# A DiT block with a routed expert layer on one core: the start of the kernel rewritten as one list per engine

## The chip, the cores and the metric

The kernel runs on 1 core of one Trainium2 chip. The metric is the device time of one execution in microseconds (us). Three runs of the kernel before took 1523.42, 1529.38 and 1528.04 us, median 1528.04.

## The reference

Everything is float32. Four batches of 1024 tokens with 256 features pass through two layers; each batch has a condition row and 77 context rows.

```python
m = silu(cond) @ w_ada + b_ada                    # nine sections of 256: shift, scale, gate x 3
h = ln(x) * (1 + sc_msa) + sh_msa
x = x + self_attn(h) * g_msa                      # 16 heads, windows of 128 tokens, shifted by 64
h = ln(x) * (1 + sc_mca) + sh_mca
x = x + topk_cross_attn(h, context) * g_mca       # 16 heads, softmax over the 16 largest of 77 scores
h = ln(x) * (1 + sc_mlp) + sh_mlp
x = x + swiglu(h) * g_mlp                         # hidden size 1024
nx = layer_norm(x, gamma, beta)                   # second layer
evidence = softmax(nx @ Wq @ (ctx @ Wk).T / 16) @ (ctx @ Wv)
combined = concat(nx, evidence, anchor)           # anchor: the condition row, the same for all tokens
routed = sum_e softmax(combined @ router_W + b)[e] * (silu(combined @ e_w1[e] + e_b1) @ e_w2[e] + e_b2)
g = sigmoid(silu(combined @ gate_w1 + gate_b1) @ gate_w2 + gate_b2)
out = x + g * (routed @ out_w + out_b)
```

## The kernel before

**Units and stages.** A unit is 256 tokens (two tiles of 128 rows); there are 16 units, four per batch. Each passes through stage A (self-attention up to the query of the cross-attention), stage C (cross-attention with its top-k) and stage B (gated MLP and experts). The loop body `both(k, r, batch)` works on B of unit k-1, C of unit k and A of unit k+1 at once. Ahead of the loop, A of units 0 and 1 and C of unit 0 must be done; a tail follows it.

**Order.** Every engine has its own instruction list, written by hand; engines meet at semaphores, and an engine that waits holds up all that is behind it on its list. The eight PSUM banks are shared by named jobs: `BANK_JOBS` gives each bank its jobs in order, and `before(name, u)` (L88) turns a name and a unit into the number of jobs that the bank had before. For the start this number comes from `PRO_ORDER` (L68 to 77), built from `FIRST_JOBS`. In the names below, `s00` to `s13` are the score jobs of stage A by tile and slot (4 slots of 4 heads), `p..` their turned probabilities, `c..` and `y..` the same of the cross-attention, `r1`, `r2` turned inverse sums.

**The start.** `prep_weights()` runs first, then `first()`, then `second()`, on TensorE (L476, L893, L935), DVE (L1727, L2073, L2106), ACT (L1330, L1346) and POOL (L1603, L1608). It holds:

- *Modulations.* TensorE turns 78 rows of biases and conditions into columns (L481), multiplies silu(cond) for four batches (4 columns of weights) with w_ada in slices of 512 columns (L488), so that the result has 4 rows and 2304 columns. DVE adds b_ada, loaded four times over, into `scores_or_ada` (L1759). Twelve transposes bring six sections to columns (L501), which DVE reads as `mods` (L1766). Gate rows are spread over 128 partitions by a product with a one-hot (L505, L520, L527) into `Gall`; POOL multiplies w_so and w_co with them (L1582). DVE multiplies the bias rows with the gates (L1774), then copies this batch's columns: modS, modC, chooseA (L1847 to L1849).
- *Bias rows in three parts.* A bias enters a token-major product as one bfloat16 product with three 16-bit parts of the row; `three_parts` (L1715) makes them on DVE: so, co, mo for four batches early, the expert rows late in `second()` (L1721 to L1724).
- *Folds.* The weights of the second layer are combined once: wk, wq turned and multiplied (MT, L559, L568), e_w2 turned (t.., L587) and multiplied with out_w (p.., L597), expert biases (b01, b2, L549), router rows (r0, r1), gates (G1 to G3, M0, M1), and the anchor's part of the first expert layer (L577, 28 products with 4 columns). They use banks 5 to 7 in turn, and DVE reads all of them, scaling some on the way, in the order of `FOLD_JOBS` (L367). One semaphore, `fold_read`, counts the reads.
- *Loads.* SP issues all of them (L380 to L439): columns, w_ada whole, x of unit 0, rows, the five attention weights, context, x of unit 1, fold weights, then (after the modulations, since they lie in the same tiles) Wm1 and W1nx, and later e_w2's third part, w_m2 and the evidence weights. w_ada borrows the tiles of W1nx and Wm1.

Stage A on TensorE is `a_turn_input` (L653), `a_k`, `a_q` (L668), `a_v` (L704), `a_scores` (L722), `a_turn_probs` (L730), `a_values` (L742), `a_turn_inverses` (L759), `a_project` (L676, L683), `a_turn_query`, `a_query`. DVE takes row maxima (L1928), ACT the exponents (L1249) and copies the turned slots (L1256). In stage C, `a_cross_scores` (L785) is copied by ACT (L1264), DVE finds the 16 largest (`a_topk`, half a and b, L1966 to L1978), POOL subtracts the maximum (`a_shift`, L1555), ACT takes the exponent (L1271), DVE keeps the chosen (`a_pick`, L1985). Stage B begins with `b_hidden` (L811), which reads hB.

## Time and profile before

| what | us |
|---|---|
| median of three runs | 1528.04 |
| the profiled execution | 1530.62 |
| its span, first to last instruction | 1528.8 |
| TensorE busy | 1456.4 (95%) |
| DVE busy | 1025.6 (67%) |
| ACT busy | 836.5 (55%) |
| POOL busy | 240.1 (16%) |
| mean granted TensorE clock | 0.968 of 2.4 GHz |

The difference of 1.8 us between the profiled execution and its span is time outside the first and last instruction. Busy shares are averages over the whole span. In the forty equal slices of the page, TensorE shows 5 in the second slice and 8 in the next three, then 9 up to the end; the granted clock reads 8, 8, 6, 6 in the first four slices and then 8 and 9.

### The profile page before, as it was taken

How to read it: one execution, taken by the hardware profiler on the slowest of the kernel's cores; microseconds unless marked ns; L12 is line 12 of the kernel's file. 1: busy time of each engine (PE TensorE's matmuls, PEld its weight loads, DVE VectorE, ACT ScalarE, POOL GpSimd, SP SyncE). 2: the span in 40 equal slices, each digit the busy share in tenths (PEclk: the TensorE clock that was granted, in tenths of full speed). 3: DMA queues.
4: the chain of work that ended last, by engine and by line, in shares of the span. 5: the costliest groups of instructions: out<-in, count | busy, mean ns of one | idle time of the engine just before them, and what ended most of it. 6: DMA issues, size and time to landing. Idle time of an engine off the chain costs nothing.

```text
span 1528.8 us, 32900 instructions
## 1 busy us (share of the span) xinstructions
PE 1456.4 (95%) x9793; PEld 1215.0 (79%) x9793; DVE 1025.6 (67%) x4678; ACT 836.5 (55%) x2546; POOL 240.1 (16%) x413
## 2 busy tenths in 40 slices
PE   5888699999999999999999999999999999999987
PEld 2656578888888888888888788888888888887876
DVE  4446685868768585867768585867768585857532
ACT  1415337574756537574756637484756637574423
POOL 2001210112123110111123110111123110111100
PEclk8866899999999999999999999999999999999999
...
DMA packets 25140, 31.70 MB, mean 21 GB/s; under 512 B 3051, under 2 KB 21627, under 8 KB 24443
## 3 DMA queue, kind: packets, MB, share of 16 engines
...
q14 instruction: 96, 0.79, 0.2%
...
## 4 chain that ended last, share of the span: by engine, by line
PE 73%; DVE 19%; issue 5%; ACT 1%; DVEq 1%; DMA 0%; POOL 0%; SPq 0%; POOLq 0%; ACTq 0%
PE bank L882 11%; PE bank L811 10%; PE bank L857 9%; PE bank L683 6%; DVE knocked L1978 5%; PE bank L864 5%; PE bank L821 5%; PE bank L668 4%; PE bank L742 4%; PE bank L730 4%; DVE M L1971 2%; PE bank L722 2%; DVE M L1966 2%; PE bank L676 2%; PE bank L639 2%
## 5 line engine op out<-in xcount | busy, mean ns | idle before, releaser
L811 PE MATMUL bank<-hB,Wm 128*128 128x256 f32 x1024 | 244.2, 385 | 3.7 <-issue 2.5
L811 PEld LDWEIGHTS bank<-hB,Wm 128*128 128x128 f32 x1024 | 191.9, 191 | 35.8 <-issue 11.9
L857 PE MATMUL bank<-nxT,W1nx 128*128 128x256 f32 x896 | 213.2, 384 | 0.0
L1249 ACT ACTIVATE prob<-bank,rmax 128x128 f32<-128x128 f32 x512 | 180.0, 435 | 32.9 <-DVE rmax L1928 32.9
L1256 ACT ACTIVATE probT<-bank 128x512 f32<-128x512 f32 (+1 forms) x256 | 141.4, 610 | 97.3 <-PE bank L795 76.0
L857 PEld LDWEIGHTS bank<-nxT,W1nx 128*128 128x128 f32 x896 | 167.2, 192 | 23.1 <-issue 2.8
L882 PE MATMUL bank<-W2p,gT 128*128 128x256 f32 x768 | 182.8, 381 | 0.0
L882 PEld LDWEIGHTS bank<-W2p,gT 128*128 128x128 f32 x768 | 144.0, 192 | 20.6
L1555 POOL TENSOR_TENSOR scores_or_ada<-scores_or_ada,M 128x308 f32<-128x308 f32 x128 | 94.8, 741 | 401.4 <-DVE knocked L1978 401.4
L1285 ACT ACTIVATE tbs<-bank,b1half 128x256 f32<-128x256 f32 x128 | 60.6, 473 | 150.9 <-PE bank L811 115.5
L1297 ACT ACTIVATE tbs<-bank,betaH 128x256 f32<-128x256 f32 x224 | 94.9, 484 | 85.7 <-PE bank L864 85.4
L1249 ACT ACTIVATION_READ_ACCUMULATOR prob<-bank,rmax 128x1 f32 x512 | 140.6, 276 | 0.0
L821 PE MATMUL bank<-Wm_g,gT 128*128 128x256 f32 x512 | 122.7, 380 | 0.0
L864 PE MATMUL bank<-wT,Vp 77*128 77x256 f32 x448 | 114.0, 383 | 0.0
L821 PEld LDWEIGHTS bank<-Wm_g,gT 128*128 128x128 f32 x512 | 96.9, 190 | 18.1 <-issue 4.2
L1978 DVE MATCH_REPLACE8 knocked<-M,scores_or_ada 128x77 f32<-128x77 f32 x512 | 108.5, 223 | 1.2 <-issue 0.8
L1978 DVE MATCH_REPLACE8 knocked<-M,knocked 128x77 f32<-128x77 f32 x512 | 108.5, 223 | 0.1
L864 PEld LDWEIGHTS bank<-wT,Vp 77*128 77x128 f32 x448 | 81.4, 190 | 14.3 <-issue 4.8
L1993 DVE SCALAR_TENSOR_TENSOR gT<-tbs,gT 128x256 f32<-128x256 f32 x128 | 55.8, 436 | 51.5 <-ACT gT L1287 51.4
L1928 DVE TENSOR_REDUCE rmax<-bank 128x4 f32<-128x512 f32 x128 | 80.7, 684 | 10.5 <-PE bank L722 10.5
L1966 DVE MAX8 M<-scores_or_ada 128x8 f32<-128x77 f32 x512 | 83.5, 225 | 4.1 <-ACT scores_or_ada L1264 4.0
L1971 DVE MAX8 M<-knocked 128x8 f32<-128x77 f32 x512 | 83.4, 225 | 0.2
...
## 6 DMA issues: line engine op xcount, KB each, us to landing
...
```

The costliest lines, as they stand in the source:

```text
L811: m = pe.matmul(bank_of(name)[:, half * UT:(half + 1) * UT], Wm1[:, k, c:c + P], hB[:, k, :], start=(k == 0), stop=(k == CB - 1))
L821: m = pe.matmul(bank_of("mo")[:, t * C:(t + 1) * C], gT[:, j, t * P:(t + 1) * P], Wm2_g[:, j, :], start=False, stop=(j == HJ - 1), skip_gr ...
L857: pe.matmul(bank_of(name)[:, n * UT:(n + 1) * UT], W1nx[:, k, c0 + n * P:c0 + (n + 1) * P], nxT[:, k, :], start=(n == 0 and k == 0), stop= ...
L864: m = pe.matmul(bank_of(name)[:, n * UT:(n + 1) * UT], Vp[:, c0 + n * P:c0 + (n + 1) * P], wT[:, :], start=False, stop=True, skip_group_ch ...
L882: m = pe.matmul(bank_of(name)[:, t * C:(t + 1) * C], hE[:, e % 2, k, t * P:(t + 1) * P], W2p[:, e * RB + k, :], start=False, stop=(k == RB ...
L1249: m = act.activation(prob[:, s, i, :], psum[s][:, i * P:(i + 1) * P], ACT.Exp, bias=rmax[:, t, s * HPS + i:s * HPS + i + 1], accum_out=rsu ...
L1256: act.activation(probT[0:np_, s], psum[s][0:np_, :].rearrange("p (i q) -> p i q", i=HPS), ACT.Copy)\
L1297: act.activation(tb[tb_of(name)][:, n * UT:(n + 1) * UT], bank_of(name)[:, n * UT:(n + 1) * UT], ACT.Tanh, bias=betaH[:, n0 + n:n0 + n + 1 ...
L1555: pool.tensor_tensor(Dx[:, t, g, :], S[:, t, g, :], M12[:, t, g, 0:1].to_broadcast([P, HPS, LC]), ALU.subtract)\
L1966: dve.max(M12[:, t, h, 0:8], S[:, t, h, :]).then_inc(topk, 1)
L1971: dve.max(M12[:, t, h, 8:TOPK], K[:, h, :]).then_inc(topk, 1)
L1978: dve.match_replace(K[:, h, :], top, src, KNOCKED).then_inc(topk, 1)
```

## The change

The first two units and all weight folds become one list per engine, `prologue()`, with an order of single slots instead of groups; `PRO_JOBS` gives the banks' order to match. The modulations are made by feature: w_ada is the stationary side, siluT (4 columns) the moving one, so they come out as columns; only the three gate sections are still made as rows. w_ada is loaded in two pieces, sections 0 and 1 first. The loads follow first use. Folds rotate through the three banks in a new order and are read by DVE or ACT, each bank with a semaphore of its own; scale factors that the reads applied are now put on out_w and the gate row once. `three_parts` moves to POOL. The loop and the tail are as before.

The diff of the fold order and of the loads, with the semaphores that SP waits on:

```diff
-ada_loads = [(Wada[k], w_ada[k * P:(k + 1) * P, :]) for k in range(CB)]
+ada_loads = [(Wada[k][:, 0:2 * C], w_ada[k * P:(k + 1) * P, 0:2 * C]) for k in range(CB)]
+ada_rest_loads = [(Wada[k][:, 2 * C:9 * C], w_ada[k * P:(k + 1) * P, 2 * C:9 * C]) for k in range(CB)]
...
+FOLD_JOBS = [
+    "cols", "mS", "cT", "cK", "cV", "g25", "g8", "bv", "G0", "mR", "t01", "t00",
+    "wq", "M0", "p01", "anchor", "p00", "t11", "t10", "b01", "p10", "p11", "G1", "b2",
+    "t20", "t21", "p21", "p20", "G2", "wk", "MT", "G3", "r0", "M1", "r1",
+]
...
+    sp.dma_start(Wqkv[:, :, :], blocks(w_qkv)).then_inc(qkv_loaded, 16)
+    load_ctx(0)
+    sp.dma_start(Wkv[:, :, :], blocks(w_kv)).then_inc(kv_loaded, 16)
+    for loads, loaded in ((ada_rest_loads, ada_rest_loaded), (rows_loads, rows_loaded), (gated_loads, gated_loaded)):
         for dst, src in loads:
             sp.dma_start(dst, src).then_inc(loaded, 16)
-    load_ctx(0)
+    sp.dma_start(Wq2[:, :, :], blocks(w_q)).then_inc(q2_loaded, 16)
     load_x(1, 1)
     for dst, src in folded_loads:
         sp.dma_start(dst, src).then_inc(folded_loaded, 16)
     sp.dma_start(ew2[:, :, :], e2_rows[:, 0:2 * RB, :]).then_inc(ew2_loaded, 16)
     for dst, src in anchor_loads:
         sp.dma_start(dst, src).then_inc(anchor_loaded, 16)
-    sp.wait_ge(init_full, 6)
+    sp.wait_ge(fold_full, max(FOLD_FULL[n] for n in ("g8", "g25", "mR")))
     for dst, src in wb_loads:
         sp.dma_start(dst, src).then_inc(wb_loaded, 16)
-    sp.wait_ge(fold_read, FOLD_JOBS.index("t01") + 1)
+    wait_read(sp, "t00")
+    wait_read(sp, "t01")
     sp.dma_start(ew2[:, 0:RB, :], e2_rows[:, 2 * RB:3 * RB, :]).then_inc(ew2_loaded, 16)
     load_x(2, 2)
     load_x(3, 3)
-    sp.wait_ge(fold_read, FOLD_JOBS.index("b2") + 1)
+    wait_read(sp, "anchor")
+    for dst, src in evidence_loads:
+        sp.dma_start(dst, src).then_inc(evidence_loaded, 16)
+    for name in ("b01", "b2", "MT", "p20", "p21"):
+        wait_read(sp, name)
     load_wm2()
-    sp.wait_ge(fold_read, FOLD_JOBS.index("anchor") + 1)
-    for dst, src in evidence_loads:
-        sp.dma_start(dst, src).then_inc(wb_loaded, 16)
...
```

The modulations on TensorE, new:

```python
def modulations(name, sections):
    pe.wait_ge(silu_ready, 1)
    if name == "mS":
        pe.wait_ge(ada_loaded, 16 * CB)
    else:
        pe.wait_ge(ada_rest_loaded, 16 * CB)
    bk = fold_bank(name)
    for n, sec in enumerate(sections):
        for f in range(CB):
            c, o = sec * C + f * P, (n * CB + f) * NB
            for k in range(CB):
                m = pe.matmul(bk[:, o:o + NB], Wada[k][:, c:c + P], siluT[:, k, :], start=(k == 0), stop=(k == CB - 1))
    m.then_inc(fold_full, 1)
def gate_sections(name, gates):
    pe.wait_ge(ada_rest_loaded, 16 * CB)
    bk = fold_bank(name)
    for n, g in enumerate(gates):
        c = (3 * g + 2) * C
        for k in range(CB):
            m = pe.matmul(bk[0:NB, n * C:(n + 1) * C], siluT[:, k, :], Wada[k][:, c:c + C], start=(k == 0), stop=(k == CB - 1))
    m.then_inc(fold_full, 1)
```

TensorE's new list (in place of `prep_weights`, `first`, `second`), after which the loop begins:

```python
def prologue():
    columns_turned()
    modulations("mS", (1, 0))
    context_turned(0, fold_bank("cT"))
    a_turn_input(0)
    context_keys(0, fold_bank("cK"))
    pe.wait_ge(qkv_loaded, 16)
    a_v(0, 0)
    a_q(0)
    a_v(1, 0)
    a_k(0)
    context_values(0, fold_bank("cV"))
    gate_sections("g25", (0, 1))
    gate_sections("g8", (2,))
    a_scores(0, range(SLOTS), 0)
    value_biases()
    fold_gates(0)
    modulations("mR", (4, 3, 7, 6))
    a_turn_probs(0, 0, 0)
    a_turn_probs(0, 1, 0)
    a_turn_probs(0, 2, 0)
    fold_turn_second(0, 1)
    a_turn_probs(0, 3, 0)
    fold_turn_second(0, 0)
    fold_turn("wq", wq_sb)
    fold_mlp_gates(0)
    a_scores(1, range(SLOTS), 0)
    a_values(0, 0)
    fold_second(0, 1)
    a_turn_probs(1, 0, 0)
    fold_anchor()
    a_turn_probs(1, 1, 0)
    a_turn_probs(1, 2, 0)
    a_turn_probs(1, 3, 0)
    a_turn_inverses("r1", "pv", 0)
    fold_second(0, 0)
    a_values(1, 0)
    fold_turn_second(1, 1)
    fold_turn_second(1, 0)
    fold_expert_biases("b01", (0, 1))
    pe.wait_ge(prepared, 1)
    pe.wait_ge(doneA, 3)
    pe.wait_ge(gatedA, 2)
    a_project("pv", oT, "so", Wso_g, 0)
    fold_second(1, 0)
    fold_second(1, 1)
    fold_gates(1)
    a_turn_query(0)
    fold_expert_biases("b2", (2,))
    fold_turn_second(2, 0)
    fold_turn_second(2, 1)
    pe.wait_ge(q2_loaded, 16)
    a_query(0)
    fold_second(2, 1)
    a_turn_input(1)
    fold_second(2, 0)
    pe.wait_ge(readA, 2)
    a_cross_scores(0, range(SLOTS), 0)
    fold_gates(2)
    fold_turn("wk", wk_sb)
    a_v(0, 1)
    a_k(1)
    a_v(1, 1)
    fold_qk()
    fold_gates(3)
    a_cross_scores(1, range(SLOTS), 0)
    fold_router_anchor()
    a_q(1)
    a_scores(0, range(SLOTS), 1)
    a_turn_probs(0, 0, 1)
    a_turn_probs(0, 1, 1)
    fold_mlp_gates(1)
    a_turn_probs(0, 2, 1)
    a_turn_probs(0, 3, 1)
    a_scores(1, range(SLOTS), 1)
    a_values(0, 1)
    a_turn_probs(1, 0, 1)
    a_turn_probs(1, 1, 1)
    fold_router_rows()
    a_turn_probs(1, 2, 1)
    a_turn_probs(1, 3, 1)
    a_turn_inverses("r1", "pv", 1)
    a_values(1, 1)
    a_turn_picked(0, 0, 0)
    a_turn_picked(0, 1, 0)
    a_turn_picked(0, 2, 0)
    a_turn_picked(0, 3, 0)
    a_project("pv", oT, "so", Wso_g, 1)
    pe.wait_ge(values_read, 1)
    a_cross_values(0, 0)
    a_turn_picked(1, 0, 0)
    a_turn_picked(1, 1, 0)
    a_turn_picked(1, 2, 0)
    a_turn_picked(1, 3, 0)
    a_turn_inverses("r2", "xv", 0)
    a_cross_values(1, 0)
    pe.wait_ge(doneC, 1)
    pe.wait_ge(gatedC, 2)
    a_project("xv", oT2, "co", Wco_g, 0)
    a_turn_query(1)
    a_query(1)
    turn("ln3", xnB, 0, normed[2], TILES)
    wait_folds(pe)
    pe.wait_ge(wb_loaded, 16 * len(wb_loads))
    pe.wait_ge(evidence_loaded, 16 * len(evidence_loads))
    pe.wait_ge(prepared_b, 1)
    pe.wait_ge(prepared, 2)
```

POOL's, with `three_parts` as it now runs there (`chain` waits for the instruction it wraps):

```python
def three_parts(np_, r0, r1, nth):
    n = r1 - r0
    cur = rows[0:np_, r0:r1, :]
    part, rest = split_b[0:np_, 0:n, :], split[0:np_, 0:n, :]
    for p in range(3):
        chain(pool.tensor_copy(part, cur))
        last = pool.tensor_copy(bias3[32 * p:32 * p + np_, r0:r1, :], part)
        if p < 2:
            chain(last)
            chain(pool.tensor_tensor(rest, cur, part, ALU.subtract))
            cur = rest
    last.then_inc(prepared, 1)
    pool.wait_ge(prepared, nth)
def prologue():
    rstd_of(0, EPS0, 0)
    pool.wait_ge(rows_gated, 1)
    three_parts(NB, 0, 3, 1)
    wait_read(pool, "G0")
    wait_read(pool, "bv")
    gate_so(0)
    rstd_of(0, EPS0, 1)
    gate_co(0)
    a_spread("pv", 0)
    rstd_of(1, EPS0, 0)
    pool.wait_ge(expert_rows, 1)
    three_parts(1, BIAS.index("e0"), len(BIAS), 2)
    a_shift(0, 0, 0)
    a_shift(0, 1, 0)
    a_shift(0, 2, 0)
    a_shift(0, 3, 0)
    a_shift(1, 0, 0)
    a_shift_kept(0, 0)
    a_shift(1, 1, 0)
    a_shift(1, 2, 0)
    a_shift(1, 3, 0)
    a_spread("pv", 1)
    a_shift_kept(1, 0)
    rstd_of(1, EPS0, 1)
    a_spread("xv", 0)
    rstd_of(2, EPS0, 0)
```

DVE's, cut to what the prediction speaks of; the rest follows the same jobs:

```python
def prologue():
    dve.wait_ge(fold_full, FOLD_FULL["cols"])
    read_done("cols", dve.tensor_copy(cols[:, :], fold_psum("cols")[:, 0:NCOL]))
    a_load(0, 0)
    ln_stats(0, xs[0], 0)
    silu()
    helpers()
    ln_apply(0, xs[0], xnA, 0)
    dve.wait_ge(fold_full, FOLD_FULL["mS"])
    read_mods("mS", 0, (1, 0))
    context_turned(0, fold_psum("cT"))
    dve.tensor_copy(modS[:, :], mods[:, 0, 0:4]).then_inc(doneA, 1)
    context_keys(0, fold_psum("cK"))
    ...
    a_load(1, 0)
    ln_stats(0, xs[1], 1)
    a_max(0, (0,), 0)
    a_max(0, (1,), 0)
    a_max(0, (2,), 0)
    dve.wait_ge(rows_loaded, 16 * len(rows_loads))
    dve.wait_ge(fold_full, FOLD_FULL["bv"])
    so_co = rows[:, 0:2, :].rearrange("b n c -> b (n c)")
    read_done("bv", dve.tensor_tensor(so_co, fold_psum("bv")[0:NB, :], so_co, ALU.add))
    a_max(0, (3,), 0)
    gate_bias_rows()
    read_fold("G0", Gall[:, 0:2, :].rearrange("p g c -> p (g c)"), fold_psum("G0")[:, :])
    dve.wait_ge(fold_full, FOLD_FULL["mR"])
    read_mods("mR", 2, (4, 3, 7, 6))
    read_fold("t01", e2T[1], fold_psum("t01")[:, :])
    dve.tensor_copy(modC[:, :], mods[:, 0, 4:8]).then_inc(doneA, 1)
    read_fold("t00", e2T[0], fold_psum("t00")[:, :])
    dve.wait_ge(folded_loaded, 16 * len(folded_loads))
    dve.tensor_scalar(outw, outw, 0.25, None, ALU.mult).then_inc(out_scaled, 1)
    ...
    dve.tensor_copy(chooseA[:, :], choose[:, 0, :]).then_inc(doneA, 1)
    prep_c(0)
    a_invert_sums(0)
    ...
    prepared_for_b()
    dve.wait_ge(fold_full, FOLD_FULL["b01"])
    expert_bias("b01", (0, 1))
    a_residual(xs[0], xs[0], "so", 0)
    wait_drained(dve, "so", 0)
    ln_stats(1, xs[0], 0)
    ...
    halve_expert_biases()
    read_fold("p21", W2p[:, 2 * RB + 2:2 * RB + 4, :].rearrange("p k c -> p (k c)"), fold_psum("p21")[:, :])
    read_fold("p20", W2p[:, 2 * RB + 0:2 * RB + 2, :].rearrange("p k c -> p (k c)"), fold_psum("p20")[:, :])
    a_topk("a", 0, 0, 0)
    a_topk("a", 0, 1, 0)
    a_topk("b", 0, 0, 0)
    a_topk("a", 0, 2, 0)
    a_topk("a", 0, 3, 0)
    a_topk("b", 0, 1, 0)
    a_topk("b", 0, 2, 0)
    a_pick(0, 0, 0)
    a_bias_queries(1)
    a_topk("a", 1, 0, 0)
    a_topk("b", 0, 3, 0)
    a_max(0, (0,), 1)
    ...
```

ACT keeps its jobs in nearly the same order, with ten fold reads among them: wq after the first four turned slots; t11, p10 and p11 after r1; t21 ahead of the query bias; G2, wk, MT and G3 around the cross-attention scores; M1 after the first turned slots of unit 1. Its exponent of the first half of tile 0 (`a_cross_exp(0, 0, 0)`) stands after `a_keys(1)` and ahead of `a_copy_values(1)` and the read of MT.

## Rows read from the trace of the kernel before

**Rows 1.** Windows: from:to, us, busy per engine (instructions), clock, DMA share, GB/s.

```profile
0.00:13.10 13.10, 0.36 (x1) 0.20 (x2) 3.03 (x15) 1.49 (x2) 3.82 (x13) 1.00 0.55 206
13.10:42.30 29.20, 24.91 (x90) 13.04 (x90) 17.11 (x42) 3.54 (x7) 4.29 (x6) 0.82 1.07 351
42.30:104.50 62.20, 50.30 (x305) 37.67 (x305) 25.20 (x55) 19.39 (x81) 2.60 (x6) 0.79 0.13 40
104.50:177.20 72.70, 51.59 (x363) 41.29 (x363) 45.97 (x239) 31.66 (x106) 14.65 (x24) 0.71 0.07 26
177.20:1528.80 1351.60, 1329.21 (x9039) 1122.78 (x9039) 934.33 (x4328) 780.46 (x2351) 214.79 (x365) 0.99 0.04 11
```

**Rows 2.** Timeline (start us, us, what), TensorE: first matmul of the loop.

```profile
177.16 3.35 PE L811 MATMUL bank<-hB,Wm 128*128 128x256 f32 x7 [1.26 <-ACT hB L1210]
```

**Rows 3.** Chain that ended last, in order of time: start us, us, what.

```profile
5.41 7.57 DMA Wm<-in_L_xcond_w_ada_dram
13.11 10.04 PE bank L488 x20
...
118.10 10.39 PE bank L577 x56
```

**Rows 4.** DMA issues: KB each, us from issue to landing.

```profile
Wm<-in_L_xcond_w_ada_dram SPq DMA_DIRECT2D x1, 1152.0 KB, 7.6
```

**Rows 5.** Timeline of DVE and ACT: first statistics, first modulation.

```profile
15.06 0.75 DVE L1900 BATCH_NORM_STATS2 stat<-x 128x6 f32<-128x256 f32 x2 [6.21 <-DMA x<-in_x_dram]
...
30.94 1.02 ACT L1210 ACTIVATE hA<-bank,modS 128x256 f32<-128x256 f32 x2 [23.72 <-DVE chooseA L1849]
```

**Rows 6.** Timeline of TensorE: the first scores.

```profile
42.27 1.15 PE L722 MATMUL bank<-km,qT 32*128 32x256 f32 x16
```

**Rows 7.** Timeline of DVE: first top-k, expert rows split, last residual.

```profile
104.55 0.66 DVE L1966 MAX8 M<-scores_or_ada 128x8 f32<-128x77 f32 x4 [4.04 <-ACT scores_or_ada L1264]
...
159.53 0.62 DVE L1721 CAST split_b<-Vp 1x1024 bf16<-1x1024 f32 x1
...
165.17 0.42 DVE L1722 COPY bias<-split_b 1x1024 bf16<-1x1024 bf16 x1
...
170.49 0.69 DVE L1953 TENSOR_TENSOR x<-x,bank 128x512 f32<-128x512 f32 x1 [4.18 <-PE bank L683]
```

**Rows 8.** Windows inside the 56 records of L577, columns as in rows 1.

```profile
118.10:120.00 1.90, 1.90 (x18) 1.90 (x18) 1.90 (x4) 1.18 (x7) 0.00 (x0) 0.97 0.00 0
120.00:122.00 2.00, 2.00 (x11) 2.00 (x11) 2.00 (x14) 2.00 (x13) 0.00 (x0) 0.50 0.00 0
```

**Rows 9.** Timeline of SP's queue: the old load of all nine bias rows.

```profile
7.69 0.49 SPq L420 DMA_DIRECT2D scores_or_ada<-in_L_xcond_b_ada_dram  x1
```

**Rows 10.** Timeline of TensorE: jobs that price the list.

```profile
23.85 1.03 PE L495 MATMUL bank<-Wco_g,bv 128*4 128x256 f32 x4
...
65.80 1.04 PE L587 MATMUL bank<-ident,gT 128*128 128x128 f32 x8
66.67 1.91 PE L730 MATMUL bank<-ident,prob 128*128 128x128 f32 x16
...
72.40 1.08 PE L742 MATMUL bank<-probT,va 128*32 128x128 f32 x32
```

**Rows 11.** Window: the busiest part of the second stretch, columns as in rows 1.

```profile
60.50:81.90 21.40, 20.36 (x129) 15.90 (x130) 8.17 (x14) 5.39 (x21) 0.74 (x2) 0.92 0.17 51
```

**Rows 12.** Timeline of POOL: two products, two copies.

```profile
27.49 1.82 POOL L1582 TENSOR_TENSOR Wso_g<-Wso_g,Gall 128x256 f32<-128x256 f32 x2 [10.07 <-DVE Gall L1770]
...
67.12 0.74 POOL L1576 COPY xnA<-rinv 128x256 f32<-128x256 f32 x2 [36.27 <-DVE rinv L1933]
```

**Rows 13.** Timeline of DVE: the bias rows of four batches, split.

```profile
27.45 2.14 DVE L1774 TENSOR_TENSOR Vp<-Vp,scores_or_ada 4x256 f32<-4x256 f32 x3
...
30.82 0.54 DVE L1721 CAST split_b<-Vp 4x768 bf16<-4x768 f32 x1
...
35.29 0.35 DVE L1722 COPY bias<-split_b 4x768 bf16<-4x768 bf16 x1
```

632 lines of the change are left out of this document (316 added, 316 removed), and 9 rows, old and new, of the table PRO_JOBS.

## The prediction

> **What bounds the kernel now.** I read the windows first. They cut the span at four marks: 42.3 us (first scores), 104.5 us (first top-k), 177.2 us (first matmul of the part that the loop repeats) and the end [rows 1]. From 177.2 us on TensorE is busy 1329.2 of 1351.6 us at a granted clock of 0.99: no room there, and the change touches none of it. Ahead of that mark it is busy 127.2 of 177.2 us at 0.71 to 0.82. So the change is worth what it does to the moment at which line 811 first runs with hB, 177.16 us [rows 2], and everything behind moves with it.
>
> Then the chain of waits, for what holds each stretch [rows 3]. TensorE waits until 13.1 us for the second half of w_ada and then spends 10.0 us on the modulations of all nine sections. The DMA issues price that wait: 1152 KB, behind as much again, landed 7.6 us after issue [rows 4]. DVE meets x only at 15.06 us, as x queues behind them, and copies modS, modC and chooseA last; ACT starts to modulate when the third is done, at 30.94 us [rows 5]. The first scores start at 42.27 us [rows 6]. Top-k starts at 104.55 us; from 159.53 to 165.6 us DVE splits four expert bias rows, with the oT product behind it on the queue, and the residual of "co" at 170.49 us is late by as much [rows 7]. TensorE gives 10.4 us to the anchor fold ahead of the turned probabilities of unit 1 [rows 3]. Within that fold the clock falls from 0.97 to 0.50 while TensorE shows no gap [rows 8].
>
> **Part 1, up to the first scores.** Removed ahead of the first modulation: seven ninths of the w_ada bytes, the 36 KB load of b_ada for four batches [rows 9], ten products of 512 or 256 columns, twelve transposes, five reads, and the gate and row products that sit before modS. SP's queue gains four issues (w_ada and b_ada in pieces) at 0.4 to 0.5 us, but Wqkv and Wkv move ahead of them. New path: the first 512 KB of w_ada are issued where the 2304 KB were. The 2304 KB took 7.6 us [rows 4], so 512 KB and the 256 KB of x take a third of that plus the time to start, which I estimate as landing at 10 us. DVE now has the statistics of x ahead of silu: 10.0 + 1.1 (stats and aggregates, from 15.06 to 16.2) + 0.35 = 11.5 us. "mS" is 8 products, 16 records. No earlier row has such products except the anchor's: 18 records in 1.90 us at 0.97, so 0.106 each, 11 in 2.00 us at 0.50, so 0.182 or more each [rows 8]: 1.7 to 3.0 us. With 0.8 us for reading them and copying modS, ACT starts at 15 to 16.5 us; I take 15.7, 15.2 earlier than now.
>
> From there to the scores took 11.3 us [rows 5, 6]. The same work stays, less 0.9 us of context keys that now fit into the wait for ACT, plus 12 records for the gate sections. Four records of 256 columns take 1.03 us with the tail that the next one covers, 0.86 from start to start [rows 10]: 2.6 us. First scores at 15.7 + 13.0 = 28.7 us, 13.6 earlier. Bounds: 26.5 (every column at full clock) and 31.
>
> **Part 2, first scores to first top-k: 62.2 us now.** TensorE's list there in records: 96 of 256 columns (bv, G0, G1, M0, b01, b2, six expert folds, so, q2) at 0.215 = 20.6 us; 72 transposes (eight slots, wq, six turns of e_w2, r1, ln2, ln1) at 0.11 [rows 10] = 7.9; three score groups 3.2 and two value groups 2.1 [rows 6, 10]. That is 33.8 us at full clock. "mR" and the anchor are 88 four-column records: 9.3 us at 0.106, 16.4 at the 0.187 that the whole anchor fold averaged (10.46 us for 56). MT, wk, both router jobs, G2, G3 and M1 leave this stretch. Since the wide work fills the waits, I take the clock of its busiest part, 0.92 [rows 11]: 36.7 + 16.4, and 3 us of waits in place of 11.9 = 56. First top-k at 28.7 + 56 = 85 us. Ends: 43.1 (all at full clock, no wait) and 67 (the clock of now, 0.79, on the wide work, 42.8, with 16.4 and 8 of waits). ACT takes ten fold reads that were DVE's, at about 0.6 each, five here and five in part 3: it was busy 19.4 of 62.2 and 31.7 of 72.7 us [rows 1], so they cost nothing unless they stand in front of a copy that TensorE wants; then one costs 0.6.
>
> New heads of queues. DVE waits for Wm1, W1nx and the rest (4.5 MB) ahead of "b01"; SP issues them only after "mR", at about 38 us (28.7, then scores, bv, G0 and mR) instead of 25. At 351 GB/s [rows 1] they land at 51; DVE gets there at about 57. Cost nothing, up to 5 us if the list runs faster than I think. POOL now splits the bias rows, and gate_so, rstd of unit 1, gate_co and the spread of the inverse sums queue behind it. No row shows POOL on so few partitions. The nearest are a product of 128x256 in 0.91 us and a copy in 0.37 [rows 12], 3.6 and 1.45 ns per column: for 768 columns 2 x 2.7 + 6 x 1.1 = 12 us, against 4.8 on DVE, from 30.82 to 35.64 [rows 13]. It starts near 36 us (28.7, four maxima, bv and the row products: 7); with two gates, rstd and the spread (5.2 together) the last ends near 53. The inverses are wanted at 50 to 54, when the anchor lets the slots be turned. I take zero, with 6 as the other end.
>
> The Trainium skill (GPSIMD Engine Reference, section 4.1 Engine selection) speaks against this move: element work belongs on VectorE, two inputs being about twice as slow on GpSimd and one input about equal. The rows differ for two inputs: 3.6 ns per column on POOL [rows 12] against 2.8 on DVE with 4x256 [rows 13] or 1.35 with 128x512. By the page the first split would take some 7 us in place of my 12, and the sum stays.
>
> **Part 3, first top-k to the loop: 72.7 us now.** Two things leave the chain: the split (159.53 to 165.6, 6.1 us) and the anchor (10.4) [rows 3, 7]. That gives 56.2. DVE has 46.0 us of work there now [rows 1], 39.5 without the split and the anchor's read, so the floor is that plus the tail that nothing shortens, 6.7 us from the residual at 170.49 to 177.16, less the 3.5 of it that is DVE work counted already: 43. Added to TensorE in this stretch are MT, wk, router, G2, G3 and M1, some 5 us, in waits of 21 us. The other end is 66.6, where only the split is saved, because the scores of unit 1 wait for a query bias that DVE now does after the first pick. That pick waits for ACT's exponent, which waits for two shifts on POOL, which stand behind the second split: 1024 columns, 16 us by the same prices, begun near 76 us, 9 before the top-k. It ends near 92, shifts and exponent at 94; the pick is due seven top-k groups (9.8 us) after 85. So it just fits, and 6 us is the price if it doesn't. First loop matmul: 85 + 56 = 141 us, against 177.2: **36 us saved**.
>
> **The loop and its loads.** w_m2 is issued after MT is read, about 95 us; its gating wants it at about 138. Evidence weights go before it and are earlier than now. Nothing there changes the loop.
>
> **The sum.** The profiled execution took 1530.62 us (span 1528.8), 2.6 above the median of 1528.04. 1530.6 - 36.2 = 1494.4; against the median 1491.8. I say 1491.5.
>
> **Rivals.** (a) *The clock holds.* Part 2 is then 43.1 + 3, and part 3 is 52, since some 14 us of TensorE work on its chain ran at 0.71: first top-k at 75, loop at 127, 50 saved: 1478. For it: busier stretches now have more clock (0.92 against 0.79) [rows 1, 11]. Against it: the clock fell inside the anchor fold with TensorE never idle [rows 8]. The Trainium skill (TensorE: Matmul & The Clock Gate, What's actually happening) has the clock follow how busy TensorE was, which would give this case; the trace disagrees for four-column products, of which the new list has 104 in place of 56. (b) *The gain is half.* In-order queues collide: part 2 keeps 8 us of waits and takes 67, part 3 takes 62: loop at 158, 19 saved: 1509. Against it, 21 us of DVE idling and 12 of TensorE's have a visible cause that the order removes. (c) *POOL becomes the bound, slower than before.* Place: the second split, in front of the first shift. At 16 us it is covered; each microsecond above 17 delays everything in part 3. From 36 us above that, 53 in all or 3.3 times the rows' price (casts to bfloat16 appear in no row of POOL), the kernel is slower; at four times, the second split alone makes it 1539. (d) *The order does nothing*: loads alone bring the first scores forward and the waits move to the same weights later. Only 4.5 MB are issued later than now and they are covered, so this is unlikely: 1525.
>
> **Chances.** Forecast (28 to 44 saved) 0.58; (a) 0.16; (b) 0.18; (c) 0.03; (d) 0.05, half of it within 0.5%, which is 7.6 us and about what a measurement of this kernel can tell from no change. Faster by more 0.94, within 0.03, slower 0.03. The range reaches to both (a) and (b), leaving their far halves out: 1473 to 1510.
>
> **What would show it.** Right: ACT's first modulation at 15 to 17 us, first scores by 31, first top-k near 85, the loop at 135 to 147, and its length still 1351 us; no DVE casts of bias rows. Wrong: POOL's splits above 17 us each with the first shift behind them, a DVE wait on the loads of Wm1 ahead of "b01", a clock at 0.5 over long busy stretches, or a loop that is longer than 1352 us, which no step here allows.

## The result, and the profile after the change

Four runs of the changed kernel took 1487.58 to 1492.47 us, median 1489.76; the kernel before, its first three runs and one more, had a median of 1526.22. The ratio is 0.976, 95% interval 0.974 to 0.978. The change saves 36.5 us; 36.2 were forecast, and 1489.8 us stands against the 1491.5 on record. The profiled execution took 1487.95 us with a span of 1485.9.

That agreement to 0.3 us is luck. Between the two profiled executions the spans differ by 42.9 us, of which 38.9 lie ahead of the loop; the profile of before was 4.4 us above its median, the one of the changed kernel 1.8 below its own. The windows of the changed kernel, cut at its own marks (first scores, first top-k, first matmul of the loop), to be read against [rows 1]:

```profile
0.00:27.80 27.80, 16.77 (x71) 13.24 (x71) 8.41 (x33) 5.04 (x9) 4.76 (x15) 1.00 0.79 253
27.80:81.80 54.00, 54.00 (x374) 45.15 (x373) 25.02 (x61) 23.14 (x86) 19.53 (x23) 0.84 0.49 170
81.80:138.30 56.50, 42.72 (x341) 32.55 (x339) 39.64 (x228) 33.89 (x111) 18.03 (x27) 0.85 0.06 20
138.30:1485.90 1347.60, 1326.08 (x9039) 1118.70 (x9039) 933.10 (x4328) 781.57 (x2351) 215.53 (x366) 1.00 0.04 11
```

Part 1 went from 42.3 to 27.8 us, part 2 from 62.2 to 54.0, part 3 from 72.7 to 56.5. In part 2 TensorE is busy in every microsecond, where it idled 11.9; what limits it there is its own work and its clock. In part 3 it still idles 13.8 us. The loop is 38.9 us earlier than at [rows 2].

The loop itself reads 1347.6 us against 1351.6, with the same 9039 matmuls. Some 1.8 us of that lie at its entry: its first eight records took 3.78 us before and 1.99 here, the lower clock level against the upper. For the rest I have no cause in the change. In the experiments below, whose loop has the same instructions, this stretch took 1347.6 to 1353.9 us from profile to profile; I count the rest as spread, without two profiles of one kernel to show it. For the same reason the marks, not the medians, decide about differences of a few microseconds.

The timeline of the changed kernel (start us, us, what), TensorE and then DVE, ACT: first modulations, first scores, anchor fold, loop; first statistics; first modulation by ACT:

```profile
11.39 0.59 PE L542 MATMUL bank<-siluT,W1nx 128*128 128x4 f32 x2 [4.76 <-DVE siluT L1892]
11.85 0.57 PE L542 MATMUL bank<-siluT,Wm 128*128 128x4 f32 x2
...
27.82 1.15 PE L780 MATMUL bank<-km,qT 32*128 32x256 f32 x16
47.04 8.40 PE L633 MATMUL bank<-condT,W1ev 128*128 128x4 f32 x56
138.29 0.91 PE L869 MATMUL bank<-hB,Wm 128*128 128x256 f32 x3 [1.26 <-ACT hB L1298]
```
```profile
9.92 0.75 DVE L2009 BATCH_NORM_STATS2 stat<-x 128x6 f32<-128x256 f32 x2 [2.93 <-DMA x<-in_x_dram]
```
```profile
16.31 1.02 ACT L1298 ACTIVATE hA<-bank,modS 128x256 f32<-128x256 f32 x2 [9.08 <-PE bank L711]
```

The chain that ended last, its start (start us, us, what). The load of x and the modulations stand where the load of w_ada and ten microseconds of line 488 stood [rows 3]. POOL's second split is on it as a whole, all eight steps from 75.63 to 86.5 us, and behind it two shifts, the exponent and the copies that ACT has queued behind that:

```profile
6.98 2.80 DMA x<-in_x_dram
11.39 3.58 PE bank L542 x16
...
75.63 1.04 POOL split_b L1744
...
82.23 2.13 POOL tbs L1748
```

The timeline of POOL: the first step of each split, the last step of the second, and the first shifts behind it:

```profile
34.04 0.81 POOL L1744 CAST split_b<-Vp 4x768 bf16<-4x768 f32 x1 [21.75 <-DVE nxT L1921]
...
75.63 1.03 POOL L1744 CAST split_b<-Vp 1x1024 bf16<-1x1024 f32 x1 [4.75 <-DVE Vp L1937]
...
85.50 1.04 POOL L1745 COPY bias<-split_b 1x1024 bf16<-1x1024 bf16 x1
86.62 2.03 POOL L1682 TENSOR_TENSOR scores<-scores,M 128x308 f32<-128x308 f32 x3
```

Eight steps take 8.7 us for 768 columns and 10.9 for 1024. The three shifts in one record behind the second split are the sign of a queue that has built up: POOL is late for all three.

### The profile page after: what moved, and what is told of

Same layout as the page of the kernel before. It is cut to its first block, busy times and chain, and to the rows that moved or that the text cites. A ratio compares the mean times of both kernels' runs of the same rounds, so it can differ in the third digit from the quotient of the medians.

```text
span 1485.9 us, 32998 instructions
## 1 busy us (share of the span) xinstructions
PE 1439.6 (97%) x9821; PEld 1209.6 (81%) x9821; DVE 1006.2 (68%) x4648; ACT 843.7 (57%) x2556; POOL 257.8 (17%) x429
## 4 chain that ended last, share of the span: by engine, by line
PE 81%; DVE 12%; issue 4%; POOL 1%; ACT 1%; DVEq 0%; SPq 0%; DMA 0%; POOLq 0%; ACTq 0%
PE bank L915 12%; PE bank L940 11%; PE bank L869 10%; PE bank L922 6%; PE bank L741 6%; PE bank L879 5%; PE bank L800 4%; PE bank L788 4%; PE bank L726 4%; DVE knocked L2087 4%; PE bank L853 3%; PE bank L780 2%; PE bank L734 2%; DVE M L2075 2%; PE bank L697 2%
## 5 line engine op out<-in xcount | busy, mean ns | idle before, releaser
L1682 POOL TENSOR_TENSOR scores<-scores,M 128x308 f32<-128x308 f32 x128 | 94.5, 739 | 371.1 <-DVE knocked L2087 371.0
L2087 DVE MATCH_REPLACE8 knocked<-M,scores 128x77 f32<-128x77 f32 x512 | 108.4, 223 | 0.7 <-issue 0.7
L1674 POOL TENSOR_SCALAR vare<-mv 128x2 f32<-128x2 f32 x64 | 14.0, 220 | 406.5 <-DVE mv L2013 404.0
L2075 DVE MAX8 M<-scores 128x8 f32<-128x77 f32 x512 | 83.5, 224 | 1.5 <-issue 0.7
```

The lines of the kernel that those rows point to most:

```text
L1682: pool.tensor_tensor(Dx[:, t, g, :], S[:, t, g, :], M12[:, t, g, 0:1].to_broadcast([P, HPS, LC]), ALU.subtract)\
L2075: dve.max(M12[:, t, h, 0:8], S[:, t, h, :]).then_inc(topk, 1)
L2087: dve.match_replace(K[:, h, :], top, src, KNOCKED).then_inc(topk, 1)
```

## The experiments

All are read at four marks, taken from each kernel's own timelines in us:

```
                              ACT modulates  scores  top-k    loop   loop to end
before                            30.94       42.27  104.55  177.16    1351.6
after                             16.31       27.82   81.78  138.29    1347.6
splits on DVE again               16.44       27.39   81.32  145.35    1353.9
old order of the loads            25.23       35.79   89.74  146.33    1349.9
all folds read by DVE             16.17       27.25   82.01  140.67    1351.6
anchor fold twice                 16.10       27.92   93.01  149.62    1350.1
silu first                        15.07       27.10   81.07  137.62    1347.6
expert rows early                 15.95       27.38   79.68  134.85    1351.4
anchor in parts                   16.01       28.18   72.53  127.13    1350.3
folds behind the so product       16.36       27.88   87.72  142.94    1349.7
the three together                14.88       26.93   76.58  131.85    1350.9
the same, rstd first              14.81       26.88   72.81  129.80    1348.2
the same, context first           13.89       27.62   73.57  129.93    1350.6
before, second split on POOL      31.22       42.66  106.05  175.25    1349.5
```

### The splits on DVE again

```diff
 # DVE
     gate_bias_rows()
+    three_parts(NB, 0, 3)
...
+    dve.wait_ge(expert_rows, 1)
+    three_parts(1, BIAS.index("e0"), len(BIAS))
     a_normalise("xv", oT2, 0)
 # POOL: both calls removed
```

> Both splits of the bias rows back on DVE, the second just ahead of the oT product. My theory (the move to POOL took them off DVE's path): the first costs DVE 4.9 us ahead of the reads of G0, mR and the turned e_w2, of which 2 to 4 reach TensorE; the second costs 6.1 on DVE's chain, and gives back the 1 to 2 us that POOL's second split now holds up ACT at 75 to 89 us. First loop matmul 6 to 9 us later than 138.3. Rival (they would be covered anyway, since DVE has 4 to 6 us waits): 0 to 2 us later. Rival (POOL is now the bound): 1 to 2 us earlier.

1500.76 us, ratio 0.983 (0.980 to 0.985): 7.1 us later than the changed kernel at the loop, and not at the top-k (0.5 earlier). So the first split is free on either engine, where 2 to 4 us were expected of it. The second, on DVE, is in front of the oT product as before [rows 7] (timelines of DVE, then TensorE):

```profile
126.02 0.67 DVE L1917 CAST split_b<-Vp 1x1024 bf16<-1x1024 f32 x1
...
131.56 0.42 DVE L1918 COPY bias<-split_b 1x1024 bf16<-1x1024 bf16 x1
132.01 0.69 DVE L2059 TENSOR_TENSOR oT<-bank,oT 128x512 f32<-128x512 f32 x1
```
```profile
133.23 3.62 PE L741 MATMUL bank<-Wco_g,oT 128*128 128x256 f32 x8
...
139.49 3.75 PE L726 MATMUL bank<-hA,Wq 128*128 128x256 f32 x8 [0.75 <-ACT hA L1298]
```

Less than half of the 7.1 us is the split itself: the oT product starts at 132.01 us and not at 128.88, 3.1 later, since it would have waited for TensorE in part anyway. The rest is clock. Behind the pause of 5.2 us TensorE ran at a granted 0.50 from 132.8 us to the loop, at 1.00 in the changed kernel, and the two groups above took 3.62 and 3.75 us where they take 1.89 and 1.96 there.

### The old kernel with its second split on POOL

```diff
 # POOL, first()
     rstd_of(0, EPS0, 1)
+    pool.wait_ge(expert_rows, 1)
+    three_parts(1, BIAS.index("e0"), len(BIAS), 2)
 # DVE, second()
-    three_parts(1, BIAS.index("e0"), len(BIAS))
     a_normalise("xv", oT2, 0)
```

> The kernel before with one part of the change alone: the second split of bias rows on POOL, behind rstd of unit 1. Theory: DVE's 6.1 us ahead of the oT product go and POOL's 11 us fit between 90.6 and 106: loop 5 to 6 us before 177.2. Rival (the parts only pay together, another wait takes its place): under 2 us.

1528.22 us, ratio 1.000 (0.999 to 1.002), and the loop only 1.9 us earlier. Part 3 is 3.5 us shorter, but the top-k comes 1.5 us later. The oT product did not move (timelines of DVE and TensorE of this kernel):

```profile
100.73 1.45 DVE L1937 TENSOR_SCALAR xnA<-x,mv,rstd 128x256 f32<-128x256 f32 x2
...
165.50 0.69 DVE L1967 TENSOR_TENSOR oT<-bank,oT 128x512 f32<-128x512 f32 x1 [3.68 <-PE bank L743]
```
```profile
156.05 3.75 PE L669 MATMUL bank<-hA,Wq 128*128 128x256 f32 x8 [0.75 <-ACT hA L1212]
```

DVE is free but TensorE is not ready. In the kernel before, the product that oT reads had been there since 162.65 us (its timeline of TensorE):

```profile
161.57 1.08 PE L742 MATMUL bank<-probT,vc 77*32 77x128 f32 x32
```

So 3.0 of the split's 6.1 us could be won there at most. Here even these were lost: the query took 3.75 us where the kernel before took 1.97, at a granted clock of 0.56 to 0.59 from 154 to 162 us, and the same product ended at 165.44. What was won is 2 us in the co product behind, which no longer starts after a pause of 3.8 us. Whether the clock was lower by the edit or by chance, one profile does not say.

Of the 1.5 us at the top-k 0.4 are there already at the first scores. The rest has a cause that neither theory had. While POOL splits (90.9 to 102.0 us), two jobs of DVE take longer: the copy of chooseC 0.77 us and not 0.18, the normalisation at 100.73 1.45 us and not 0.73. The run with rstd first, below, shows the same. So the same move is worth 0 to 2 us in the old order and 7 in the new one.

### The old order of the loads

```diff
 # SP
+    (ada_rest_loads)
     load_x(0, 0)
-    Wqkv; load_ctx(0); Wkv; ada_rest_loads
     rows_loads; gated_loads
+    Wqkv; Wkv; Wq2; load_ctx(0)
-    Wq2
```

> Order of the loads as before (all of w_ada, then x, rows, so and co, then Wqkv, Wkv, Wq, context), with all else new. Theory: x lands at 14 to 15 us instead of 9.9 and silu stands behind it on DVE, and Wqkv lands near 19; mS starts at 16, first scores 4.5 to 6 us later, and the delay runs through to the loop undiminished: first loop matmul 4.5 to 6 later. Rival (slack behind the first scores swallows it, as folds fill the waits): first scores late by 5, loop late by less than 2.

1497.42 us, ratio 0.982 (0.979 to 0.984). ACT's first modulation comes 8.9 us later, and each later mark 8.0: nothing on the way takes the delay up, and it is larger than the 4.5 to 6 that I had expected. x reaches DVE at 16.84 us and not at 9.92, and silu stands behind its statistics, so TensorE's modulations wait for x; behind them TensorE waits another 1.85 us, for the context, which the old order loads last (timeline of TensorE):

```profile
18.32 0.59 PE L544 MATMUL bank<-siluT,W1nx 128*128 128x4 f32 x2 [11.78 <-DVE siluT L1894]
...
23.73 0.52 PE L663 MATMUL bank<-ident,ctx_sb 77*128 77x77 f32 x2 [1.85 <-DMA ctx_sb<-in_ctx_dram]
```

The context, needed ahead of the turn of xnA, is what sets ACT's start here. So of the 14.5 us that part 1 gained, some 8 would be lost again with the old loads under the new lists. How the gain splits between loads and modulations under the old lists, this run does not show.

### All folds read by DVE

```diff
 # ten read_fold calls go from ACT's list to DVE's, each near its old place
-    act: read_fold("wq", ...), "t11", "p10", "p11", "t21", "G2", "wk", "MT", "G3", "M1"
+    dve: the same
```

> All ten fold reads of ACT put back on DVE, at the places where their jobs fall. Theory: DVE is the denser engine from 81.8 us on; five reads of 0.6 there cost 2.5 to 3.5 us at the loop, the five before cost 0 to 1. Rival (ACT's queue was the one that held things, as the chain of waits runs through its reads of MT and G3 at 89 to 90 us): loop within 1 us of 138.3 or earlier.

1494.26 us, ratio 0.979 (0.977 to 0.981); the loop is 2.4 us later, of which 0.2 before the top-k; the theory had 2.5 to 4.5. Five of the ten reads fall into part 2 and are nearly free there. The other five, 0.6 us each, fall into part 3, where DVE is busy 39.6 of 56.5 us, and 2.2 of their 3 us reach the loop, if the spread from profile to profile is left aside.

### The anchor fold twice

```diff
-    for n in range(W1B):
+    for n in list(range(W1B)) * 2:
```

> The anchor fold's 28 products done twice (112 records instead of 56), same result. Theory: it lies wholly on TensorE's chain and at 1.2 GHz: 56 more records at 0.187 to 0.2 cost 8 to 11 us at the loop, and the granted clock of the whole stretch reads 0.50 after its first 2 to 4 us though TensorE shows no gap. Rival (it fills waits): under 4 us. Rival on the clock (it follows how busy TensorE is): the second half of the stretch reads 1.0 and costs 5.9.

1501.02 us, ratio 0.985 (0.982 to 0.987). The top-k comes 11.2 us later and the loop 11.3. The second 56 products cost more than the first's 8.4 us, though they do the same (timeline and windows of this kernel):

```profile
47.15 20.07 PE L633 MATMUL bank<-condT,W1ev 128*128 128x4 f32 x112
```
```profile
50.00:60.00 10.00, 10.00 (x55) 10.00 (x55) 0.35 (x1) 1.13 (x5) 0.73 (x2) 0.57 0.36 101
60.00:66.00 6.00, 6.00 (x29) 6.00 (x30) 0.00 (x0) 0.00 (x0) 0.00 (x0) 0.50 0.01 3
```

The clock reads 1.00 for the fold's first 3 us and more, falls at about 51 us and then stays at the lower level until the fold ends, with TensorE busy throughout, as in [rows 8]. The rival, that it follows how busy TensorE is and is back for the second half, is refuted. All of it is on the path: in part 2 nothing can hide a TensorE instruction.

### The six folds in one block

```diff
 # TensorE; DVE's reads of the same folds move with them
     a_values(0, 0)
-    fold_second(0, 1)
     a_turn_probs(1, 0, 0)
-    fold_anchor()
...
-    fold_second(0, 0); fold_turn_second(1, 1); fold_turn_second(1, 0); fold_expert_biases("b01", (0, 1))
...
     a_project("pv", oT, "so", Wso_g, 0)
+    fold_second(0, 1); fold_anchor(); fold_second(0, 0); fold_turn_second(1, 1)
+    fold_turn_second(1, 0); fold_expert_biases("b01", (0, 1))
```

> The changed kernel with one piece of its order undone: the six folds that stand between the slots of unit 0's attention (p01, anchor, p00, t11, t10, b01; 15 to 17 us of TensorE) go in one block behind the so product, and their reads by DVE go with them. Same instructions, same banks. If the order is what filled TensorE's waits (it was busy for all of part 2's 54.0 us, where the kernel before idled 11.9 of 62.2), the waits for the turned copies, the inverse sums and the values come back: first top-k 6 us later (4 to 9), at 88, and the loop with it, near 144. Rival, that the order does little and the loads and cheaper modulations are all of part 2: top-k within 1.5 us of 81.8. Second rival: the waits come back, but the block then has a better clock and the anchor runs at 2.4 GHz after TensorE has rested: only 2 to 3 us later.

1494.70 us, ratio 0.978 (0.975 to 0.981). The top-k is 5.9 us later, as the order theory said; the loop is 4.7 later. The idle time is back between the slots (timeline of TensorE), 3.95 us between 27.5 and 90 us where the changed kernel has none up to its top-k. The other 2 us are the same work done more slowly; from 27.5 to 50 us the granted clock is 0.79 against 0.85:

```profile
46.47 0.66 PE L788 MATMUL bank<-ident,prob 128*128 128x128 f32 x4 [1.57 <-ACT prob L1337]
```

### The anchor fold in parts, behind the first top-k

```diff
-def fold_anchor():
+def fold_anchor(n0, n1):            # 14 groups of 4 records, run in six parts
...
     a_scores(0, range(SLOTS), 1)
+    fold_anchor(0, 5)
     a_turn_probs(0, 0, 1)
     a_turn_probs(0, 1, 1)
+    fold_anchor(5, 6)
...
     a_values(0, 1)
+    fold_anchor(6, 8)
     a_turn_probs(1, 0, 1)
+    fold_anchor(8, 9)
     a_turn_probs(1, 1, 1)
+    fold_anchor(9, 10)
...
+    fold_anchor(10, W1B)
     a_cross_values(0, 0)
```

The router's folds r0 and r1, which read it, and the evidence loads behind it move back as well; p00, t11, t10, b01 and M1 move up.

> The anchor fold leaves the stretch before the top-k and is done in six parts where TensorE waits for turned slots of unit 1; p00, t11, t10 and b01 take its first place. Theory: 8.2 us leave the first place, 3 of them come back as a wait for exponents; of the 8 us put into the later stretch, 4 to 5 fall into its waits. First top-k 5 to 8 us earlier, loop 3 to 5 earlier. Rival (TensorE is the bound there too): loop within 1 us. Rival (the later stretch is DVE's alone): loop 7 to 8 earlier. Clock: if short runs of four-column products among others leave it at 2.4 GHz, the 56 records take 6.0 in all instead of 8.4.

1479.56 us, ratio 0.969 (0.966 to 0.971), against 0.976 of the changed kernel. The top-k is 9.3 us earlier and the loop 11.2, more than any theory had: the fold now lies in TensorE's waits of part 3, and both parts have a better clock. Windows, part 2 and part 3:

```profile
28.18:72.50 44.32, 42.98 (x318) 34.46 (x317) 24.14 (x55) 22.63 (x86) 19.46 (x23) 0.92 0.46 160
72.50:127.10 54.60, 45.29 (x396) 36.41 (x394) 39.43 (x232) 33.23 (x111) 16.11 (x25) 0.91 0.16 54
```

The granted clock is 0.92 and 0.91 where the changed kernel has 0.84 and 0.85, so that part 3 is 1.9 us shorter although it holds 56 records more. Part 2 is 9.7 us shorter, more than the fold's 8.4: in the changed kernel the clock stayed at 0.50 for 5.6 us behind the fold (below), which costs the wide work there another 2.8, and 1.3 us come back as waits.

### The expert rows early

```diff
 # TensorE (DVE's expert_bias calls move up in the same way)
     fold_second(0, 1)
+    fold_expert_biases("b01", (0, 1))
+    fold_expert_biases("b2", (2,))
 # POOL
     a_spread("pv", 0)
-    rstd_of(1, EPS0, 0)
     pool.wait_ge(expert_rows, 1)
     three_parts(1, BIAS.index("e0"), len(BIAS), 2)
+    rstd_of(1, EPS0, 0)
```

> The expert bias products (b01, b2) move ahead of the anchor fold, so that POOL's second split runs at 52 to 63 us, where POOL is idle, and not at 75.6 to 86.5 in front of the first shifts. Theory (what the chain of waits shows there is a tie: DVE's list of seven top-k groups ends at 91.5 in any case): loop at most 1 us earlier. Rival (POOL's split is the bound of that stretch, since ACT holds four jobs behind the exponent that waits for it): loop 3 to 5 us earlier, first query product of unit 1 at 87 instead of 90.7.

1488.17 us, ratio 0.974 (0.972 to 0.977). The loop is 3.4 us earlier, of which 2.1 already at the top-k. The first shift now runs in the gap of the top-k and no longer behind the split (timeline of POOL):

```profile
81.24 0.70 POOL L1680 TENSOR_TENSOR scores<-scores,M 128x308 f32<-128x308 f32 x1 [11.53 <-DVE knocked L2085]
```

From top-k to loop that is 55.2 us in place of 56.5: POOL's lateness had cost 1.3, against the at most 1 of the theory and the 3 to 5 of its rival. The rest was won ahead of the top-k, 0.4 before the scores and 1.7 in part 2. There TensorE has no gap in either kernel, and the granted clock is 0.87 in place of 0.84: that is the same work, and the 1.7 us are clock.

### silu ahead of the statistics of x

```diff
-    a_load(0, 0)
-    ln_stats(0, xs[0], 0)
     silu()
     helpers()
+    a_load(0, 0)
+    ln_stats(0, xs[0], 0)
```

> silu and its helpers stand ahead of the wait for x on DVE. Theory: TensorE's mS waited 4.8 us for silu, which waited for x at 9.9 us though it needs nothing of it; mS now starts when the first 512 KB of w_ada land, at 8.5 to 9 us, and everything up to the loop comes 2 to 2.7 us earlier. Rival (the loads of Wqkv or the normalised x hold the next step): first scores 0 to 1 us earlier. Rival (slack further on): scores earlier by 2.5, loop by less than 1.

1487.87 us, ratio 0.975 (0.972 to 0.978). The modulations start at 8.41 us in place of 11.39, but only 1.2 of these 3.0 us reach ACT and 0.7 the scores. The next wait is right behind (timeline of TensorE):

```profile
8.41 0.56 PE L542 MATMUL bank<-siluT,W1nx 128*128 128x4 f32 x2 [1.88 <-DMA Wm<-in_L_xcond_w_ada_dram]
...
13.57 0.52 PE L661 MATMUL bank<-ident,ctx_sb 77*128 77x77 f32 x2 [1.62 <-DMA ctx_sb<-in_ctx_dram]
```

### The three gains together, twice

> The changed kernel with three edits at once: the anchor fold in parts behind the first top-k (alone: loop 11.2 us earlier), the expert bias rows made early so that their split on POOL ends before the first shift is due (alone: 3.4), silu ahead of the statistics of x (alone: 0.7). Theory: with the anchor out of part 2 the top-k starts at 72.5 us, but POOL splits until 77.3 and its first three shifts run behind that, so the early split is worth at least what it was alone: loop at 127.1 - 3.4 - 0.7 = 123.0 us (121 to 124.5), first shift within 2 us of the top-k, 1474 to 1476 us. First rival: after the anchor's move TensorE and not POOL is what the start of part 3 waits for (busy 45.3 of 54.6 us there, against 42.7 of 56.5): the split gives 1 us or less, loop at 125.5 to 126.5. Second rival: b01 and b2 before the turned slots of tile 1 push the inverse sums back and DVE waits for the weights of the second layer, as these are asked for sooner: top-k no earlier than 73.5, loop at 127 or later.

1485.17 us, ratio 0.972 (0.970 to 0.974): worse than the anchor in parts alone, top-k at 76.58 and loop at 131.85. On POOL the split ran from 52.7 to 63.7 us ahead of rstd, whose input was ready at 59.9. With the anchor fold gone from that place nothing covers it. The marks are those of the second rival, but not by its cause (timeline of DVE):

```profile
64.98 0.73 DVE L2025 TENSOR_SCALAR xnA<-x,mv,rstd 128x256 f32<-128x256 f32 x2 [5.04 <-POOL rstd L1682]
```

So rstd went back in front of the split:

> The three edits together as before, but on POOL the inverse deviation of unit 0's second norm (rstd, 0.22 and 0.72 us) stands ahead of the split of the expert rows and no longer behind it. Theory: in the run of the three together POOL was in the split from 52.7 to 63.7 us while the variance lay ready at 59.9, DVE waited 5.04 us for rstd, and the first top-k came at 76.6 instead of 72.5. Without that the top-k is back at 72 (71.3 to 72.8); the split runs from 61 to 72, its shifts from 73.5 instead of 77.4, and the loop begins at 127.1 - 3.4 - 0.7 = 123.0 us (122 to 124.5). Rival: TensorE (busy 45.3 of 54.6 us in part 3 of the run with the anchor in parts alone) holds part 3 by now: loop at 125.5 to 126.5 although the shifts are earlier.

1480.96 us, ratio 0.970 (0.969 to 0.972). The top-k is back at 72.81, the wait for rstd is 1.26 us, the first shift is at 74.45 and not at 77.36. Yet the loop starts at 129.80, not at 123, and 2.7 us behind the kernel with the anchor in parts alone. Nor is it the 125.5 to 126.5 of the rival. Three things are seen.

First, at the first scores this kernel is 1.3 us ahead of the one with the anchor in parts, and at the top-k 0.3 behind it. The split now runs at 61.1 to 72.0 us, and DVE's two normalisations fall into it (timeline of DVE):

```profile
61.16 2.19 DVE L2025 TENSOR_SCALAR xnA<-x,mv,rstd 128x256 f32<-128x256 f32 x2 [1.26 <-POOL rstd L1682]
```

They took 2.19 and 2.76 us. In the kernel with the anchor in parts, where POOL is idle at that moment, they took 0.73 and 0.72. It is the slowing that the old kernel showed with its split on POOL.

Second, the early shifts win next to nothing. In both kernels DVE is busy almost without a gap from the top-k to 96 us, and there TensorE's list is at most 0.5 us ahead of the other's. That points to DVE, and neither to POOL nor to TensorE, as what holds this stretch.

Third, most of the 2.7 us is clock. Windows of this kernel, and then of the kernel with the anchor in parts:

```profile
88.80:96.80 8.00, 6.42 (x36) 5.05 (x36) 8.00 (x62) 7.48 (x32) 1.41 (x2) 0.50 0.00 1
96.80:104.80 8.00, 8.00 (x67) 6.97 (x60) 5.16 (x21) 6.66 (x34) 1.12 (x3) 0.50 0.02 3
104.80:112.80 8.00, 8.00 (x73) 7.07 (x71) 3.64 (x16) 4.94 (x10) 0.92 (x2) 0.77 0.00 1
112.80:120.80 8.00, 7.66 (x103) 7.04 (x102) 3.44 (x15) 2.85 (x5) 1.69 (x4) 0.79 0.48 158
```
```profile
88.50:96.50 8.00, 5.76 (x29) 4.50 (x33) 8.00 (x58) 7.95 (x35) 1.41 (x2) 0.56 0.00 1
96.50:104.50 8.00, 6.89 (x76) 5.40 (x68) 5.63 (x25) 6.19 (x34) 0.70 (x1) 0.80 0.01 3
104.50:112.50 8.00, 6.96 (x76) 6.06 (x74) 4.49 (x18) 5.18 (x11) 1.34 (x3) 1.00 0.00 1
112.50:120.50 8.00, 7.66 (x109) 6.69 (x110) 3.23 (x13) 2.52 (x5) 1.69 (x4) 1.00 0.61 218
```

The order of the list is the same in both. Here the clock stays at the lower level longer, TensorE fills its waits and is 1.2 us behind at the so product. Then it falls a second time, 16 turns at 115.2 us take 3.63 us and not 1.97, and it is 2.7 behind. All three kernels with the gains together have 0.79 to 0.82 in part 3, the anchor in parts alone 0.91; each is one profile. Why the clock rose at one time here and later there the runs do not settle.

### The context ahead of Wqkv

```diff
     load_x(0, 0)
+    load_ctx(0)
     (Wqkv)
-    load_ctx(0)
```

> The same kernel as the one with rstd first, but the context of batch 0 is loaded ahead of Wqkv instead of behind it. TensorE waited 1.30 us, until 13.39, for the context in the run of the three together, and right behind it, at 13.70, turns xnA. If the context alone held it, the turn comes 1 us or more earlier, ACT's first modulation at 13.9 instead of 14.9, and every mark with it by 0.8 to 1.2. Rival: xnA is only ready at 13.5 or so and Wqkv comes 0.5 us later: modulation at 14.7 to 15.0, the first scores where they were or 0.5 us later.

ACT's first modulation moved by 0.9 us, to 13.89, as the theory said. But the first scores came 0.7 us later (27.62). Wkv, now last of the three, held TensorE 1.16 us, so that the context's keys start at 14.93 and not at 14.64; the other 0.45 us is the query product at 18.48, 3.07 us and not 2.62. The gain went to the next load in the queue and the delay to a slower product; the loop is at 129.93 and the ratio is 0.970 (0.969 to 0.972).

## Why the prediction was right, and where its terms were off

**Part 1** (28.7 forecast, 27.8 measured). x was expected at 10.0 us and met at 9.92; siluT was read at 11.39, where the sum had 11.5. From there the recorded sum does not add up: 11.5, 1.7 to 3.0 and 0.8 give 14.0 to 15.3 us, not 15 to 16.5. ACT started at 16.31 all the same, because two terms were too small. The 16 records of "mS" took 3.58 us and not 1.7 to 3.0, and from their end to ACT's start it took 1.34 and not 0.8, as the turns of the context and of xnA stand in between. The upper price of a record, 0.182 us, was a window divided by its count [rows 8]. A window also counts a record that only reaches into it: seven windows over this fold count 66 records where there are 56. The records at 11.85 us and behind start 0.43 us apart for two, 0.213 each. From ACT's start to the scores took 11.5 us, not 13.0; the gate sections took 2.68 as forecast (2.6), but 24 records of query, key and value took 6.4 us where they took 8.4 before, at a better clock. The errors, 0.6 one way and 1.5 the other, cancel in part, by luck.

**Part 2** (56 forecast, 54.0 measured). The four-column records, 88 with "mR" (5.0 us) and the anchor (8.4), took 13.4 us and not 16.4. No wait was left, where I had kept 3. The wide work then had 40.6 us, 3.9 more than its 36.7. The fall of the clock inside the four-column records reaches into the wide work behind them, 4.0 us behind "mR" and 5.6 behind the anchor (windows of the changed kernel):

```profile
36.90:40.90 4.00, 4.00 (x21) 4.00 (x21) 1.07 (x5) 1.79 (x3) 3.79 (x4) 0.53 0.70 227
...
55.40:61.00 5.60, 5.60 (x23) 5.15 (x23) 0.69 (x4) 2.39 (x4) 0.00 (x0) 0.50 0.62 208
61.00:81.80 20.80, 20.80 (x145) 15.46 (x143) 9.95 (x22) 5.87 (x12) 6.84 (x7) 1.00 0.09 33
```

That costs 4.7 us, where the 0.92 taken from the old kernel's busiest part had allowed 2.9. The other 2.1 are the list and its prices; G2, which I had put into part 3, is 1.0 of them. So two errors of 3 us in the four-column records and the waits met one of 3.9 in the wide work. And one of the signs that were to show the forecast wrong, a clock at 0.5 over long busy stretches, did come, from about 51 to 61 us, while the time came out right. The forecast that ACT's reads, the loads of Wm1 and W1nx (issued from 36.9 us, forecast 38) and the first split cost nothing held: the inverse spread at 51.13 waited for DVE and not for POOL, and DVE's longest waits were for TensorE.

**The splits on POOL** (12 and 16 us forecast, 8.7 and 10.9 measured). Here the term failed. I priced a copy from POOL's 128x256 row and let the ratio of columns carry it. The Trainium skill (GPSIMD Engine Reference, 4.1 Engine selection) has operations of two inputs about twice as slow on GpSimd as on VectorE, and those of one input about equal. For two inputs POOL's 2.12 us for 1024 columns stand against DVE's 1.21, which is 1.75 times and agrees roughly. For one input its 1.03 stands against 0.67 for the cast and 0.42 for the copy (both in the run with the splits on DVE), 1.5 and 2.5 times, so that part of the rule does not hold here. The estimate from the page, about 7 us for the first split, was 1.7 below the 8.7 measured; mine was 3.3 above.

**Second split "just fits"**. It began at 75.6 as forecast (76) and ended at 86.5 instead of 92, and the first pick did not wait for it. Yet it was not free: it stands on the chain that ended last, the shifts behind it ran late, and moving it earlier gave 1.3 us in part 3. "The pick is due" was the wrong test; the exponent and the slots of unit 1 follow the shifts too.

**Part 3** (56.2 forecast, 56.5 measured) is right in its sum, while one of the two steps was worth less than was taken off for it. I subtracted 6.1 us for the split and 10.4 for the anchor from the chain of before. From the top-k to the end of the values product that oT reads it took 58.1 us before and 47.0 now: 11.1 less, the anchor and a little more. From there to the loop it took 14.5 and now 9.5, 5.0 less. Of these only 3.0 are the wait behind the split; most of the other 2 is the co product, which now runs at the full clock. Put back into the new kernel the split cost 7.1, 3.1 of wait and 4 of clock; taken from the old one alone it gave 2. The chain of before lists what ended each wait, not what would have ended it next.

**The rivals.** "The order does nothing" is refuted by the run with the folds in one block (5.9 us). "The gain is half" and "POOL is the bound" did not come. "The clock holds" (75 and 127 us at the two marks, 1478) is what the kernel with the anchor in parts reached, with 72.5, 127.1 and 1479.6: that case needed the anchor's four-column records out of part 2, so it is another kernel that meets these numbers, and not the rival's claim about this one, whose clock in part 2 was 0.84. The last test on record, a loop of 1351 us, was too strict: it varies by 6 us between profiles of the same loop code.
